# The layers' norm: weight and bias on ScalarE, and a group's mean behind the feed-forward products

## The reference

```python
def ffn_layer(x, g, bln, W1, b1, W2, b2):
    mu = x.mean(-1, keepdims=True)
    var = ((x - mu) ** 2).mean(-1, keepdims=True)
    xn = (x - mu) / jnp.sqrt(var + 1e-05) * g + bln
    hg = xn @ W1 + b1
    a, gate = jnp.split(hg, 2, -1)
    return a * jax.nn.gelu(gate, approximate=False) @ W2 + b2

for i in range(DEPTH):    # 6
    x = attn_layer(shift_tokens(x), Wqkv[i], q_scale[i], k_scale[i], Wo[i]) + x
    x = ffn_layer(shift_tokens(x), ln_g[i], ln_b[i], W1[i], b1[i], W2[i], b2[i]) + x
```

## Time and profile before

| | us |
|---|---|
| median of three runs | 3920.88 |
| lowest and highest | 3917.01, 3927.07 |
| profiled execution, own time | 3918.71 |
| its span in the trace | 3916.9 |
| TensorE busy | 3581.4 (91%) |
| VectorE busy | 3162.1 (81%) |
| ScalarE busy | 2652.5 (68%) |
| GpSimd busy | 2432.0 (62%) |

### The profile page before, as it was taken

One profiled execution on the slowest core, in us unless ns is written; L12 is line 12 of the kernel. 1 busy time (PEld: TensorE's weight loads), 2 busy tenths in 40 slices (PEclk: granted clock), 3 DMA queues, 4 the chain that ended last, 5 costly groups with the idle time before them and its releaser, 6 DMA issues.

```text
span 3916.9 us, 146395 instructions
## 1 busy us (share of the span) xinstructions
PE 3581.4 (91%) x60128; PEld 2226.2 (57%) x60128; DVE 3162.1 (81%) x4377; ACT 2652.5 (68%) x4972; POOL 2432.0 (62%) x2197
## 2 busy tenths in 40 slices
PE   5676776899999999999999999999999999999997
PEld 2222222566666666666666666666666666666664
DVE  4899998888878778888878788778787887888884
ACT  3555554677777777767776777677777777676765
POOL 0355554876666666666666666666666666666661
PEclk9889898999999999999999999999999999999999
DMA  3000000111111111111110111111111111110101
GB/s 76 0 0 0 0 0 0 34 32 31 31 42 41 34 30 31 31 47 38 35 32 26 42 42 36 32 31 31 45 37 33 31 31 47 36 36 27 32 28 37
DMA packets 64418, 120.05 MB, mean 31 GB/s; under 512 B 18196, under 2 KB 35986, under 8 KB 63634
## 3 DMA queue, kind: packets, MB, share of 16 engines
q1 hardware_dynamic: 63762, 110.70, 9.7%
HBM read 20.50 MB, written 2.10 MB: 6 GB/s over the span
## 4 chain that ended last, share of the span: by engine, by line
PE 53%; DVE 15%; issue 9%; ACT 7%; POOL 0%; ACTq 0%; DMA 0%; DVEq 0%; POOLq 0%; SPq 0%
PE ob L1187 10%; PE qk L1129 9%; PE sc L1214 7%; PE trb L1001 6%; PE vob L1195 4%; PE vob L1135 4%; PE sc L1163 4%; DVE arena L888 3%; PE sc L1221 3%; DVE ssq L894 3%; DVE mx L901 3%; PE ob L1001 2%; DVE arena L889 2%; ACT arena L619 2%; DVE xnT L978 1%
## 5 line engine op out<-in xcount | busy, mean ns | idle before, releaser
L507 POOL TENSOR_TENSOR arena<-arena,rnorm 128x512 f32<-128x512 f32 x768 | 793.7, 1054 | 929.3 <-ACT rnorm L626 928.8
L500 POOL TENSOR_TENSOR arena<-arena 128x512 f32<-128x512 f32 x768 | 961.7, 1274 | 84.9 <-DVE arena L889 84.9
L633 ACT ACTIVATE arena<-trb 128x512 f32<-128x512 f32 x768 | 465.7, 606 | 432.4 <-PE trb L1001 432.4
L1129 PE MATMUL qk<-wqkv,xs 128*128 128x512 f32 x1536 | 734.2, 601 | 16.0 <-issue 8.9
L888 DVE TENSOR_TENSOR arena<-qk,tab_q 128x512 f32<-128x512 f32 x384 | 263.7, 687 | 504.6 <-ACT arena L619 499.6
L483 POOL TENSOR_TENSOR arena<-arena 128x512 f32<-128x512 f32 x256 | 299.9, 1180 | 345.4 <-DVE arena L858 329.9
L1001 PE MATMUL trb<-ident,arena 128*128 128x128 f32 x3072 | 483.0, 280 | 10.7 <-ACT arena L633 7.6
L619 ACT ACTIVATE arena<-qk 128x512 f32<-128x512 f32 x768 | 433.5, 592 | 79.4 <-PE qk L1129 65.5
L1129 PEld LDWEIGHTS qk<-wqkv,xs 128*128 128x128 f32 x1536 | 294.5, 193 | 312.0 <-issue 294.8
L894 DVE TENSOR_REDUCE ssq<-arena 128x16 f32<-128x1024 f32 x384 | 464.3, 1209 | 0.0
L514 POOL TENSOR_TENSOR arena<-arena,rinv 128x512 f32<-128x512 f32 x384 | 392.4, 1043 | 65.8 <-DVE rinv L911 65.8
(11 more groups left out here) (139 smaller groups left out, 6020.5 us busy)
## 6 DMA issues: line engine op xcount, KB each, us to landing
arena<-arena SPq DMA_DIRECT2D x192, 384.0 KB, 3.2
arena<-arena SPq DMA_DIRECT2D x192, 64.0 KB, 3.0
wqkv<-in_L_ffn_Wqkv SPq DMA_DIRECT2D x18, 512.0 KB, 4.3
wo<-in_L_ffn_Wo SPq DMA_DIRECT2D x6, 512.0 KB, 4.0
arena<-in_L_attn_x SPq DMA_DIRECT2D x8, 256.0 KB, 2.8
out<-arena SPq DMA_DIRECT2D x8, 256.0 KB, 2.2
w<-in_L_ffn_W SPq DMA_DIRECT2D x6, 341.0 KB, 2.9
arena<-in_sel SPq DMA_DIRECT2D x1, 1024.0 KB, 5.0
```

The lines of the kernel that those rows point to most:

```text
L500: nc.gpsimd.tensor_tensor(ts[c * 2 + j][:, heads], tu[:, 0, heads], tu[:, 1, heads], ALU.add).then_inc(summed[0], 1)
L507: nc.gpsimd.tensor_tensor(part, part, rnorm[j][:, 8 * h:8 * h + 8].unsqueeze(2).to_broadcast([P, 8, HEAD]), ALU.mult) \
L633: A((qT, kT)[j][u][:, 4 * h:4 * h + 4, at_col:at_col + P], TRB.rearrange("p (a t) -> p a t", a=4), ACT.Copy) \
L1129: MM(QK[:, 512 * h:512 * h + 512], lhsT=xs[u][:, c * P:(c + 1) * P], rhs=wqkv[:, col:col + 512], start=True, stop=True) \
```

## The change

Two edits. In slot 6 VectorE only multiplies the centred tokens with the inverse root, before the square sums and not after them, and ScalarE applies weight and bias as scale and bias of one activation, behind the exponential and before the logarithm. In slot 3 TensorE makes the mean after the up products of the slot and not before them.

```diff
@@ ScalarE, layer_slot
                 at_ = step_at(l, k, LAG_SCORES)
                 if at_:
                     exps(*at_)
+                at_ = group_at(l, k, LAG_NORMED)
+                if at_:
+                    item(act_e, ln_aff, at_[1])
+                    A(xnT[:, at_[0] * GROUP:at_[0] * GROUP + GROUP], xc[0], ACT.Identity, scale=lpar[:, 0:1], bias=lpar[:, 1:2]).then_inc(ln_out[0], 1)
                 if unit:
                     norms(*unit)
@@ VectorE, layer_slot
-                if unit:
-                    square_sums(*unit)
                 at_ = group_at(l, k, LAG_NORMED)
                 if at_:
...
                     item(dve, ln_rstd, at_[1] + 2 * GROUPS)
-                    V.scalar_tensor_tensor(out=xc[0], in0=xc[0], scalar=lpar[:, 0:1], in1=rstd[0], op0=ALU.mult, op1=ALU.mult) \
-                        .then_inc(ln_aff[0], 1)
-                    item(dve, ln_aff, at_[1])
-                    V.tensor_scalar(xnT[:, at_[0] * GROUP:at_[0] * GROUP + GROUP], xc[0], lpar[:, 1:2], None, ALU.add).then_inc(ln_out[0], 1)
+                    V.tensor_tensor(xc[0], xc[0], rstd[0], ALU.mult).then_inc(ln_aff[0], 1)
+                if unit:
+                    square_sums(*unit)
@@ TensorE, layer_slot
-                if mean:
-                    pe.wait_ge(ln_in[0], mean[1] + 1)
-                    if out_before:
-                        item(pe, x_added, out_before[0])
-                    MM(VOB[:, :], lhsT=meanw[:], rhs=xs2.rearrange("p s t -> p (s t)"), start=True, stop=True).then_inc(ln_mean[0], 1)
...
                         up(*at_, parts, scored)
+                if mean:
+                    pe.wait_ge(ln_in[0], mean[1] + 1)
+                    if out_before:
+                        item(pe, x_added, out_before[0])
+                    MM(VOB[:, :], lhsT=meanw[:], rhs=xs2.rearrange("p s t -> p (s t)"), start=True, stop=True).then_inc(ln_mean[0], 1)
```

## The result

The changed kernel takes 3875.34 us (median of 4 runs, 3872.14 to 3877.08), the kernel before in the same rounds 3922.95 us (3917.01 to 3927.07). The ratio is 0.9879, with a 95% interval from 0.9862 to 0.9896. The forecast was 3870 us, and its range, 3856 to 3891 us, holds the time. The profiled execution of the changed kernel took 3875.7 us, its span is 3873.8 us against 3916.9 us before, and its granted clock is 0.98 as before.

A forecast was written before the change was run, and what follows sets the result against it. TensorE was taken to bound the kernel, busy 505.05 of 520 us, so only its idle time could be gained. 1.03 + 0.10 us in 45 groups, 51 us, gave 3868 for the profiled execution and 3870 us for the median, range 3856 to 3891.

The forecast's parts named there:

- the two waits: TensorE's idle time: 57.7 us before the mean product (for L918), 10.8 us before the up product (for L978).
- Slot 3, 1.03 us gained of 1.49: Mean behind the up products: 1.03 of 1.49 us stall goes; 0.46 becomes the value product's wait for VectorE's mean subtraction.
- The release and the late start: Slot 3: value product starts 0.06 us after the mean's subtraction ends; its successor follows after 0.96 us, not 0.86.
- Slot 5 holds with 0.16 us to spare: Slot 5's variance product, coming 1.03 us earlier, still finds VectorE's addition L918 released 0.16 us before.
- In slots 4 to 6 I find no other wait as close: No wait in slots 4 to 6 as close as slot 5's, so the 1.03 us arrive at slot 7.
- Slot 7, 0.10 us gained: Slot 7: the 0.42 us wait for xnT goes, ScalarE's later copy L633 holds the second turn; gain 0.10, bounds 0 to 0.25.
- VectorE's product 0.68 us: Slot 6: VectorE's remaining product of two tiles takes 0.68 us, as L955 does, and doesn't stretch.
- A group of 64.8 us: Sign in the profile after: a group of 512 tokens takes 64.8 us, against about 66 before.
- The sum, 45 x 1.13 = 51 us: Whole kernel: 1.03 plus 0.10 us a group, in 45 of the 48 groups, gives 51 us.
- Both stalls: First rival: the stalls of slots 3 and 7 go entirely, 86 us gained, 3835 us; chance 0.08.
- the second rival: A further wait of 0.5 us or more in slots 4 to 6 gives back most of slot 3's gain: 3888 to 3907 us; chance 0.12.
- the point where it loses: Last rival, ScalarE bounding slot 7: the change loses from 1.78 us more on ScalarE; 3940 us at 2.2; chance 0.09.

The follow-up runs named there:

- the norm edit alone: Against the kernel before, only the slot 6 change, with ScalarE applying weight and bias; the mean stays ahead of the up products: 3906.11 us, 0.9967.
- both reorderings: Changed kernel, with VectorE's mean subtraction ahead of the rotary products and ScalarE's copy of the turned tile ahead of the GELUs: 3850.79 us, 0.9816 of before.

## Why the prediction was right, and where it was not

- **TensorE bounds, and the two waits are what can be gained:** right. TensorE's idle time fell from 15 to 8 us of 520, and the waits for L918 and L978 are gone in the steady groups.
- **Slot 3, 1.03 us gained of 1.49 and 0.46 left in a new wait:** right in mechanism and size. The slot's stall is 0.46 us; the undisturbed group is 1.04 us shorter by this edit alone; VectorE's subtraction did not move with TensorE. The release and the late start, 0.06 and 0.10 us, measured 0.05 and 0.11.
- **Slot 5 holds with 0.16 us to spare:** right in every steady group; the variance product waits for VectorE's addition once, 0.6 us, while the pipeline empties.
- **"In slots 4 to 6 I find no other wait as close":** wrong. Slot 4's scores wait 13 times, 5.6 us, for instructions, and the values in slot 3 17 times, 9.4 us. I had looked at waits between engines only; five of this kind were in the trace of before, in slot 7, with two falls of the clock behind them, and no step of the prediction has either.
- **Slot 7, 0.10 us gained:** 0.08 by the norm edit alone. ScalarE's new step lasted 0.83 us where I took 0.75, within the bounds. The step right behind it came 0.75 us later, not 0.65, and the release of the turn took 0.13 us, not 0.06; with these two the gain should have been nothing. It was there because the copy came only 0.64 us later (measured from the slot's key product): ScalarE's two squares (L619) had held a pause for TensorE, 1.17 us for the pair in the kernel before and 1.08 after, and it swallowed 0.1. So the size was right by errors that cancel. By the figures of the Trainium skill, "ScalarE: Activation LUTs", section "What ACT_TABLE_LOAD costs", it was an estimate of 0.80 us and 3873 us for the kernel: the row is 4% above the page's figure and nearer to it than to mine. The time, 3875.34, is nearer too, but that is chance, as slot 7 is under 1 us of what the sum missed.
- **VectorE's product 0.68 us, without stretching:** 0.68. **A group of 64.8 us:** 64.86.
- **The sum, 45 x 1.13 = 51 us:** the spans differ by 43.1. Of the 7.8 us between, 1.1 are a 45th group, since there were 44 with something to lose; 44 x 0.02 = 0.9 are slot 7; 2.7 are the disturbances in the 39 groups, 13.9 us for 11.2; 2.2 the five groups with a pass's end, which gained 3.4 us and not 5 x 1.11 = 5.6, mainly since the waits at the jump grew from 8.9 to 10.5 us (the clock fell at three jumps in both); and 0.9 the later start. So the size was off by terms outside the regular group, all on one side. The third of these is a balance: the kernel before lost some 8 us to waits in its groups and 3.4 to the clock, the kernel after 13.9 to waits alone. The medians differ by 47.6 us; that they come nearer to 51 than the spans is the spread of single executions, a few microseconds on either side.
- **The rivals.** Both stalls didn't go entirely; each of the two new waits was shown to be real, by taking it away. Nothing was given back in slot 5; in slots 3 and 4 the disturbances took 0.07 us a group more than before (2.7 us in 39), far under the second rival's 0.5. ScalarE's chain does set slot 7's pace, but at 0.83 us it is below the point where it loses. The rule of the Trainium skill, "ScalarE: Activation LUTs", section "Rules for kernel authors", that additions and multiplications belong on VectorE did not decide here: L978 took 1.29 us on VectorE at the median, and the step 0.83 us on ScalarE.

What stays open: why the norm edit takes away the five waits for instructions in slot 7 with the same products in the same order, and so whether some 11 of its 14 us come from VectorE's lighter load; and why a wait of over 1 us is followed by a fall of the clock in one execution or group and not in another. Neither was tried apart.

## What to carry to other kernels

Where an engine stalls in front of work that has its inputs, put that work first, and then count the stall of the next reader of the same buffer: here 0.46 of 1.49 us came back that way, and could be worked out beforehand from rows. Read the waits that no other engine ends as well, and measure a loop by its undisturbed pass and by the sum above it: a gain in the schedule can be eaten by disturbances that it calls up (30 us of schedule gave 19). Before you explain a few microseconds, look at the granted clock of the very groups that differ: one fall was 1.7 us here. In a queue that many wait for, put the short step that frees a buffer ahead of longer ones that nobody waits for yet, here the GELUs; that was worth 23 us, half as much as the whole change.

## What the runs showed of the hardware

- TensorE waits for its instructions in dense runs of small products: up to 0.8 us at a time and 14.1 us in all after the change, up to 1.3 us with both reorderings, at positions that repeat every 256 instructions and move with the instruction count alone (16 turns more ahead of the layers moved each of them by 16 products).
- A loop's jump back costs TensorE a wait of 2.1 to 3.9 us for instructions; the step out of the loop costs nothing that shows (64.98 us, a plain group).
- Beside waits for instructions of 1.1 us and more TensorE's clock fell to 1.2 GHz for 3.4 us at a time, now and then for 6.8; one fall made a group 1.7 us longer.
- 64 tiny products ahead of the layers, 1.85 us of work, move 10 us out of the groups and put 15 us to the loop's jumps and to the start.
- A second operand per partition adds 0.09 us to a ScalarE step of 128x512 (742 to 833 ns).
- VectorE's scalar step of the earlier trace rows took from 0.49 to 1.36 us for the same work, whereas the product of two tiles, 0.68 us, varied by 14 ns over 48 executions.
